# Projecting all queries first in a fused attention and FFN kernel

## The reference, cut to what matters

```python
x = x + xattn(layernorm(x), ctx, mask, Wq, bq, Wk, bk, Wv, bv, Wo, bo)
# att = scale * q k^T;  att * mask - 1e10 * (1 - mask);  softmax;  @ v;  @ Wo + bo
t = layernorm(x)
h = relu(t @ w1[0] + b1[0]);  y = t + h @ w2[0] + b2[0]
x = x + layernorm(y) * gamma + beta
```

## Time and profile before

| | us |
|---|---|
| median of 3 runs (lowest, highest) | 248.0 (247.46, 249.1) |
| the profiled execution, device time | 246.66 |
| its span, first to last instruction | 244.9 |
| TensorE busy | 208.8 (85%) |
| VectorE busy | 149.8 (61%) |
| ScalarE (ACT) busy | 120.9 (49%) |
| GpSimd busy | 80.2 (33%) |
| mean granted TensorE clock | 0.941 |
| moved by DMA | 26.09 MB |

### The profile page before, as it was taken

One profiled execution on the slowest core, in us unless ns is written; L12 is line 12 of the kernel. 1 busy time (PEld: TensorE's weight loads), 2 busy tenths in 40 slices (PEclk: granted clock), 3 DMA queues, 4 the chain that ended last, 5 costly groups with the idle time before them and its releaser, 6 DMA issues.

```text
span 244.9 us, 3545 instructions
## 1 busy us (share of the span) xinstructions
PE 208.8 (85%) x1273; PEld 159.0 (65%) x1273; DVE 149.8 (61%) x354; ACT 120.9 (49%) x210; POOL 80.2 (33%) x88
## 2 busy tenths in 40 slices
PE   0378779459968999996999999999999999889990
PEld 0273757145613775484779876898777899878890
DVE  1989478836651697442338865826858426885464
ACT  2442932326636447677632648744755850158200
POOL 5627617130410041824101732321541441460010
PEclk9999955959995799999999999999999999999998
DMA  6963679857767707593072434000410100011011
GB/s 180 364 212 77 182 175 244 223 173 190 174 152 215 167 19 130 139 197 118 5 160 78 111 66 107 3 3 26 106 45 4 43 0 3 0 43 43 3 43 43
DMA packets 18098, 26.09 MB, mean 107 GB/s; under 512 B 2441, under 2 KB 9393, under 8 KB 18081
## 3 DMA queue, kind: packets, MB, share of 16 engines
q1 hardware_dynamic: 15024, 20.85, 34.5%
q10 hardware_dynamic: 3057, 5.02, 6.9%
HBM read 14.92 MB, written 8.72 MB: 97 GB/s over the span
## 4 chain that ended last, share of the span: by engine, by line
PE 61%; DMA 14%; DVE 12%; SPq 3%; issue 3%; ACT 2%; ACTq 2%; POOL 1%; POOLq 0%
PE T L674 7%; PE acc L686 6%; DMA Sq<-nmx 5%; PE W L736 5%; PE W L738 5%; PE M L654 5%; PE W L737 5%; PE W L753 4%; PE W L750 4%; PE W L751 4%; DMA Sq<-mD 3%; PE W L695 3%; SPq L520 2%; DMA xin<-in_x_dram 2%; DMA Mq<-qh 2%
## 5 line engine op out<-in xcount | busy, mean ns | idle before, releaser
L839 ACT ACTIVATE PT<-T 77x512 f32<-77x512 f32 x64 | 35.1, 592 | 35.8 <-PE T L674 28.3
L750 PE MATMUL W<-w2h,hh 128*128 128x256 f32 x128 | 36.5, 285 | 0.4 <-ACT hh L883 0.4
L994 DVE TENSOR_REDUCE mx<-M 128x6 f32<-128x462 f32 (+1 forms) x48 | 26.1, 580 | 17.4 <-PE M L654 17.1
L753 PE MATMUL W<-w2h,hl 128*128 128x256 f32 x128 | 36.2, 283 | 0.2 <-DVE hl L1057 0.2
L751 PE MATMUL W<-w2l,hh 128*128 128x256 f32 x128 | 36.0, 281 | 0.0
L674 PE MATMUL T<-Sq,KS 128*77 128x512 f32 x64 | 26.2, 470 | 6.3 <-ACT PT L839 3.7
L879 ACT ACTIVATE hr<-W,cols 128x512 f32<-128x512 f32 x32 | 22.1, 689 | 12.3 <-PE W L738 11.1
L654 PE MATMUL M<-KM,Mq 128*128 128x234 f32 (+1 forms) x96 | 21.3, 346 | 7.6 <-DMA Mq<-qh 6.5
L736 PE MATMUL W<-x2h,w1h 128*128 128x512 f32 x64 | 26.3, 410 | 1.5 <-DVE x2l L1051 1.5
L654 PEld LDWEIGHTS M<-KM,Mq 128*128 128x128 f32 (+1 forms) x96 | 17.9, 240 | 13.7 <-DMA Mq<-qh 7.9
L1176 POOL TENSOR_TENSOR hl<-hr,hh 128x512 fp32r<-128x512 f32 x12 | 15.5, 1288 | 33.0 <-ACT hh L883 33.0
(11 more groups left out here) (138 smaller groups left out, 408.0 us busy)
## 6 DMA issues: line engine op xcount, KB each, us to landing
Sq<-qD SPq DMA_DIRECT2D x16, 384.0 KB
qD<-qh ACTq DMA_DIRECT2D x16, 256.0 KB
xin<-in_x_dram SPq DMA_DIRECT2D x4, 512.0 KB, 8.6
qD<-ql SPq DMA_DIRECT2D x8, 256.0 KB
Mq<-qh SPq DMA_DIRECT2D x16, 96.0 KB, 4.5
out_dram<-xn SPq DMA_DIRECT2D x6, 256.0 KB, 2.2
Sq<-mD SPq DMA_DIRECT2D x1, 1280.0 KB, 8.2
w1raw<-in_L_ffn_w_dram SPq DMA_DIRECT2D x2, 512.0 KB, 8.8
```

Of the source, the lines that this page charges most:

```text
L750: e.matmul(y, hh[:, f, q:q + 128], w2h[:, f * E:(f + 1) * E], start=(f == 0), stop=False)
L753: i = e.matmul(y, hl[:, f, q:q + 128], w2h[:, f * E:(f + 1) * E], start=False, stop=(f == 7))
L839: e.activation(PT[:, m % 6, :], T[m % 2][0:TK, :], ACT.Exp).then_inc(exped, 1)
L994: e.tensor_reduce(heads, M[(nth[step] - 1) % 2][:, 0:w * KP].rearrange("p (g h t) -> p g h t", g=1 if s < 2 else 2, t=KP)[:, :, :, 0:TK], ...
```

## The change

- `x` and the output are laid out so that a partition holds four consecutive rows of a chunk (one packet of 4 KB for each partition); `x` of all chunks is loaded at the start.
- Biases, identity tables and the query bias come in one constant array of 476 columns made on the host, and the context comes already turned; the loads of biases, their turn (`rows`) and the context's (`ctx`) are gone. Constants, context, Wk and Wv are the first loads on ACT's queue.
- The query bias is added inside `qproj` by a third matmul against the mask's flag rows; `bqk` and the `single`, `low` tables are gone. `keys` are plain selections: one matmul per head for `KM` and two for `KS`, 48 in all (before 56).
- `norm`, `scale`, `turn` and `qproj` of all four chunks stand ahead, among the key tables and the maxima of chunk 0; `qh` has four slots, `xn` and `xnT` two per chunk parity. SP issues one write of the high part and one (`qlow`) of the low part per group; ACT issues none.
- `qD` holds two parts per head instead of three; a quad is two transfers (32 rows of high and low, and 16 of high again). For chunks 1 to 3 `qload` fetches the copy for the maxima from `qD`.
- `mxt` turns all 16 heads at once for chunks 1 to 3. The mask reload is in two halves per tile.
- `finish` is split into `centre` and `finish`. `kh` is made by ACT from PSUM.
- The table `TIMES` is new on every engine.

The diff, cut to its core:

```diff
-        "qproj": "14.2 16.0 / 34.3 36.5 / 56.5 58.8 / 88.6 107.1",
...
+        "qproj": "14.7 19.1 / 24.8 27.0 / 29.4 31.4 / 37.0 39.9",
+        "smax": ("22.4 22.6 24.4 26.8 28.9 29.2 33.3 34.9 35.1 36.8 38.9 39.2 / 42.1 42.3 43.2 43.9 45.3 45.7 46.2 46.7 "
+            "47.1 47.6 49.0 49.2 / 56.1 57.4 57.9 59.1 60.7 66.5 67.3 68.8 71.1 73.6 76.4 76.7 / 79.7 80.3 82.0 85.4 "
+            "91.4 91.6 95.0 95.3 102.3 104.2 106.8 107.0"),
+        "mxt": "36.0 42.7 / 50.8 / 85.6 / 110.5",
+        "st": ("39.4 39.6 41.8 42.5 43.4 43.6 45.5 46.0 46.9 47.3 49.4 49.7 50.5 51.2 53.0 53.3 / 54.5 54.7 56.4 56.6 "
+            "57.6 58.2 58.8 60.5 63.9 64.1 65.6 66.2 67.1 69.0 69.2 70.4 / 89.1 89.3 90.9 91.1 94.8 95.5 96.9 100.1 "
+            "100.3 102.1 102.5 103.9 107.2 110.9 111.6 113.6 / 119.2 120.8 122.9 124.7 128.3 128.5 131.7 132.0 135.2 "
...
+        "qproj": "22.4 30.4 / 31.0 31.5 / 32.2 40.7 / 45.3 62.6",
+        "qlow": "21.8 27.1 / 29.9 32.8 / 34.4 44.7 / 93.2 125.7",
+        "qload": "19.5 23.8 / 39.6 41.3 / 52.8 57.6 / 77.1 78.2",
+        "quadq": "35.0 37.8 43.0 47.0 / 50.8 54.5 58.7 60.9 / 79.3 81.5 92.1 100.6 / 113.1 114.8 128.1 132.4",
+        "quadm": "37.3 38.9 44.2 46.4 / 52.3 53.9 57.0 62.0 / 86.9 87.5 91.6 101.7 / 112.6 114.2 125.2 133.5",
+        "finish": "126.3 129.4 / 154.4 161.2 / 195.9 197.8 / 201.8 204.1 204.6 207.2",
...
-    if kind in ("qproj", "qload", "mxt", "attn"):
+    if kind == "mxt":
+        return [[(kind, c, g) for g in range(turns(c))] for c in range(NC)]
+    if kind in ("qproj", "qlow", "qload", "attn"):
...
+def turns(c):
+
+    return 2 if c == 0 else 1
...
-        mD = dram("mD", (QR, 1024))
-        qD = [dram(f"qD{c}", (H, 3, D, 512)) for c in range(NC)]
-
-        cst = sb("cst", [P, 164])
...
-        x_v = x.rearrange("b (n p) e -> p (b n) e", p=P)
-        o_v = out.rearrange("b (n p) e -> p (b n) e", p=P)
+        x_v = x.rearrange("b (m p n) e -> p (b m) n e", m=2, n=4)
+        o_v = out.rearrange("b (m p n) e -> p (b m) n e", m=2, n=4)
...
-            e.dma_start(xin[:, 0:4, :], x_v[:, 0:4, :]).then_inc(ld_x[0], 16)
-            e.dma_start(cst[:, :], const).then_inc(ld_c, 16)
-            e.dma_start(mrow[:, :, :], mask[0, 0].rearrange("(n p) t -> p n t", p=P)).then_inc(ld_m, 16)
+            e.dma_start(xin[:, 0:4, :], x_v[:, row0(0)]).then_inc(ld_x[0], 16)
+            e.dma_start(mrow[:, :, :].rearrange("p (m n) t -> p m n t", m=2),
+                        mask[0, 0].rearrange("(m p n) t -> p m n t", m=2, n=4)).then_inc(ld_m, 16)
+            e.dma_start(xin[:, 4:8, :], x_v[:, row0(1)]).then_inc(ld_x[1], 16)
             e.dma_start(wq[:, :, :], wview(Wq)).then_inc(ld_wq, 16)
-            e.dma_start(xin[:, 4:8, :], x_v[:, row0(1):row0(1) + 4, :]).then_inc(ld_x[1], 16)
+            for c in (2, 3):
+                e.dma_start(xin[:, 4 * c:4 * c + 4, :], x_v[:, row0(c)]).then_inc(ld_x[c], 16)
             for i in range(2):
...
                 elif kind == "qproj":
                     c, g = a
-                    qd = qD[c][8 * g:8 * g + 8]
+                    fresh.wait_ge(q_high, nth[step])
+                    e.dma_start(qD[c][8 * g:8 * g + 8, :, 0, :].rearrange("h d n -> (h d) n"),
+                                qh[:, 2 * (c % 2) + g, :].bitcast(F32)).then_inc(qh_out[2 * (c % 2) + g], 16)
+                elif kind == "qlow":
+                    c, g = a
                     fresh.wait_ge(q_split, nth[step])
-                    e.dma_start(qd[:, 1, :, :], ql[:, g, :].bitcast(F32)).then_inc(q_out[g], 16)
+                    e.dma_start(qD[c][8 * g:8 * g + 8, :, 1, :].rearrange("h d n -> (h d) n"),
+                                ql[:, g, :].bitcast(F32)).then_inc(ql_out[g], 16)
...
                 elif kind == "qload":
                     c, g = a
...
+                        e.dma_start(Mqf[Q0:Q0 + 32, 4 + g, :], qh[96:P, g, :].bitcast(F32)).then_inc(ms_ld[g], 16)
+                    else:
+                        fresh.wait_ge(qh_out[2 * (c % 2) + g], 16 * (c // 2 + 1))
+                        fresh.wait_ge(scored, nth["smax", c - 1, 3, 1])
+                        e.dma_start(Mqf[Q0:Q1, 2 * g:2 * g + 2, :],
+                                    qD[c][8 * g:8 * g + 6, :, 0, :].rearrange("(j h) d n -> (h d) j n", j=2)
+                                    ).then_inc(ms_ld[g], 16)
+                        e.dma_start(Mqf[Q0:Q0 + 32, 4 + g, :],
+                                    qD[c][8 * g + 6:8 * g + 8, :, 0, :].rearrange("h d n -> (h d) n")).then_inc(ms_ld[g], 16)
...
                 elif kind == "quadq":
                     c, k = a
                     u, s = quad(c, k), 4 * (k % 2)
...
+                        fresh.wait_ge(sq_static, 4 * u + 4)
+                    else:
                         fresh.wait_ge(st_made, 4 * (u - 1))
-                    e.dma_start(Sqf[QR:P, s:s + 4, :],
-                                qD[c][4 * k:4 * k + 4].rearrange("h r d n -> (r d) h n")).then_inc(sq_ld[u % 2], 16)
+                    heads = qD[c][4 * k:4 * k + 4]
+                    e.dma_start(Sqf[Q0:Q0 + 32, s:s + 4, :], heads.rearrange("h d r n -> (d r) h n")).then_inc(sq_ld[u % 2], 16)
+                    e.dma_start(Sqf[Q0 + 32:Q1, s:s + 4, :],
...
                 elif kind == "qproj":
                     c, g = a
                     fresh.wait_ge(xnT_made, 2 * nth["turn", c])
                     fresh.wait_ge(ld_wq, 16)
                     t = take(step)
-                    e.matmul(t[:, :], wq[:, 0, g * 128:(g + 1) * 128], xnT[:, 0, :], start=True, stop=False)
-                    e.matmul(t[:, :], wq[:, 1, g * 128:(g + 1) * 128], xnT[:, 1, :],
+                    e.matmul(t[:, :], wq[:, 0, g * 128:(g + 1) * 128], xnT[:, c % 2, 0, :], start=True, stop=False)
+                    e.matmul(t[:, :], wq[:, 1, g * 128:(g + 1) * 128], xnT[:, c % 2, 1, :], start=False, stop=False)
+                    fresh.wait_ge(bqr_made, 1)
+                    fresh.wait_ge(mT_made, half(c) + 1)
+                    e.matmul(t[:, :], bqr[:, g, :], mT[:, 512 * half(c):512 * half(c) + 512],
                              start=False, stop=True).then_inc(q_made, 1)
...
+                        fresh.wait_ge(*((km_made, m - 2) if m < 9 else (ks_made, m - 8)))
+                    fresh.wait_ge(*((k_high, g + 1) if to == "KM" else (k_split, g + 1)))
+                    for i, h in enumerate(range(3 * j, min(3 * j + 3, 8))):
+                        o = t[0:48, 2 * TK * i:2 * TK * (i + 1)]
                         high = kh[:, g, :, :].rearrange("p b t -> p (b t)")
-                        e.matmul(o, single[0:TK, 8 * g + h, :], low[0:TK, :, :].rearrange("p b t -> p (b t)"),
-                                 start=True, stop=False)
                         if to == "KM":
-                            i = e.matmul(o, once[:, h, :], high, start=False, stop=True)
+                            made = e.matmul(o, sel_m[:, h, :], high, start=True, stop=True)
                         else:
-                            e.matmul(o, twice[:, h, :], high, start=False, stop=False)
-                            i = e.matmul(o, once[:, h, :], kl[:, g, :, :].rearrange("p b t -> p (b t)"),
-                                         start=False, stop=True)
-                    i.then_inc(keys_made, 1)
...
                 elif kind == "mxt":
                     c, g = a
-                    fresh.wait_ge(maxed, 12 * c + (12 if g else 8))
+                    r = H // turns(c)
+                    fresh.wait_ge(maxed, 12 * c + (8 if turns(c) == 2 and g == 0 else 12))
                     t = take(step)
                     for n in range(4):
-                        i = e.transpose(t[0:8, n * 128:(n + 1) * 128], mx[:, n, 8 * g:8 * g + 8], ident)
+                        i = e.transpose(t[0:r, n * 128:(n + 1) * 128], mx[:, c % 2, n, r * g:r * g + r], ident)
                     i.then_inc(mx_turned, 1)
...
                 elif kind == "qproj":
                     c, g = a
+                    r = 2 * (c % 2) + g
                     fresh.wait_ge(q_made, nth[step])
-                    if c:
-                        fresh.wait_ge(q_out[g], 48 * c)
-                    fresh.wait_ge(x_turned, 2 * nth["turn", c])
-                    e.copy(qh[:, g, :], bank[step][:, :]).then_inc(q_high, 1)
-                    fresh.wait_ge(q_high, nth[step])
-                    for r in (0, 2):
-                        e.dma_start(qD[c][8 * g:8 * g + 8][:, r, :, :], qh[:, g, :].bitcast(F32)).then_inc(q_out[g], 16)
+                    if c > 1:
+                        fresh.wait_ge(qh_out[r], 16)
+                        fresh.wait_ge(q_split, nth["qproj", c - 2, g])
+                    if c == 2:
+                        fresh.wait_ge(ms_ld[g], 48)
+                    e.copy(qh[:, r, :], bank[step][:, :]).then_inc(q_high, 1)
...
                 elif kind == "mxt":
                     c, g = a
+                    r = H // turns(c)
...
-                elif kind == "finish":
```

(20 more changed lines are left out.)

517 lines of the change are left out of this document (243 added, 274 removed), and 171 rows, old and new, of the table TIMES.

## The result

The changed kernel takes **231.6 us** (median of 4 runs, 230.83 to 232.05) beside 248.3 for the kernel before (247.46 to 249.1): ratio **0.9325, 95% interval 0.9284 to 0.9367**, 16.7 us less. The forecast was 223.2 us, range 214 to 232. So the sign held, and the range too, by 0.4 us at its upper end; 8.4 us are missing. The profiled execution took 232.05 us, its span is 230.2.

What follows compares the result with a forecast made beforehand. It took DMA, VectorE and waits to bound the head and TensorE, with holes, the body. Head 46.5, body 168.9 and tail 4.7 make 220.1 us; 1.76 outside the span and 1.3 to the median give 223.2, range 214 to 232.

Steps and rivals of the forecast that it cites:

- Head: Start to first score matmul: VectorE's list, then the maxima's transfer, set it; 46.5 us, 6.2 less than before.
- (b): Head, bound by bytes: 10.0 MB moved before the first score matmul, at 205 GB/s 48.7 us.
- Rival 2: Head not shortened: work added to VectorE and queues eats the gain, 52.7 us stays, total 229.4; chance 0.15.
- rival 1: Head: SP's queue drowns in query transfers ahead of the maxima, total 249 to 251 us, slower than before; chance 0.03.
- projections moved (-8.7): Body: chunks 2 and 3 no longer projected there, where TensorE is saturated; 4.35 us saved for each.
- one turn (-1.3): Body: chunks 1 to 3 turn their maxima once instead of twice, three blocks of 0.44 us less.
- ACT's issue and the half clock (-7.7): Body: ACT issues no query writes, so waits for exponentials (3.2 us) and the half clock after (4.5 us) go.
- the low part of x (-1.5): Body: TensorE's 1.5 us wait for chunk 3's low part goes, by splitting centre from finish and reordering; 0 to -1.5.
- the tail's centring (-0.5): Tail: one VectorE step, the centring, now lies beside GpSimd's root, saving 0.5 us.
- DMA for the second attention chunk (+2, range 0 to +10): Body, 46 to 70 us: 5.95 MB at 205 GB/s take 29 us, 5 late, partly beside matmuls.
- The second way: Whole kernel: the code's table of due times plus 9 us lag, with tail and rest, gives 221.4 us.
- Rivals 2 and 3: 2: head not shortened, 229.4 us, chance 0.15; 3: TensorE at half clock from 40 to 75 us, +8, 231 us, chance 0.13.

Runs made afterwards that it cites:

- Experiment 9: Maxima of chunks 1 to 3 turned in two halves again, on the version with on-chip mask copies: 223.17 us, beside 221.46 for its pair.
- Experiment 8: Chunk 3's norm, scaling, turn and projection put later, behind the first scores, on the version with on-chip mask copies: 224.58 us, ratio 0.907.
- experiment 7: Kernel before the change without its mask reload, so part of the computation is left out: 244.69 us, ratio 0.9863.
- Experiment 6: Kernel before the change with only the writes of the queries' high part issued by SP instead of ACT: 251.93 us, ratio 1.0178.
- experiment 5: Changed kernel with the writes of the queries' high part issued by ACT again, one per group: 232.15 us, ratio 0.9374.
- experiment 10: Changed kernel with the centring joined to the finish again, behind GpSimd's root: 237.54 us, beside 231.65 for its pair.
- experiment 1: Changed kernel without the mask reload, chunks 2 and 3 using the first half's mask (part of the computation left out): 221.23 us, ratio 0.8947.
- experiment 3: Changed kernel with the second half's mask rows copied on chip by GpSimd instead of reloaded by DMA: 221.73 us, and 221.46 us run again.
- Experiment 4: Changed kernel with the mask reload written to all 128 partitions instead of 77, 3.67 MB instead of 2.2: 238.1 us, ratio 0.9588.

## Why the prediction was right, and where it was wrong

**The time.** The range held at its edge, and partly by luck. The forecast gave the profiled execution 221.9 us, and it took 232.05, 10.1 more: 11.5 us missing in the body, 1.7 given back by the head. The median then lies 0.4 us below that execution, where the forecast put it 1.3 above, which gives back as much again and says nothing about the change. The stretch that the forecast held likeliest, 217 to 228, was missed. Of its signs, the first score matmul (44.8), the queries' writes off ACT, the exponentials (no wait) and the tail (just under 5 us) came as said. The granted clock of 1.0 from 60 us on and the body of 166 to 172 us did not.

**Head: right, 44.8 for 46.5, with one term too long.** The last maximum of the first eight heads, SP's issue of the transfer, and the first score matmul:

```profile
40.62 0.48 DVE L1005 TENSOR_REDUCE mx<-M 128x4 f32<-128x308 f32 x1
42.41 0.71 SPq L570 DMA_DIRECT2D Sq<-nmx  x1
44.81 0.43 PE L689 MATMUL T<-Sq,KS 128*77 128x512 f32 x1
```

VectorE's part ends at 41.1 us (the sum has 40.9). From SP's issue on it is 2.4 us, where the sum has 0.6 and 4. The bytes of (b) were right as well: 226 GB/s over 44.8 us are 10.1 MB, forecast 10.0, but the rate of 205 was too low, so its 48.7 us did not bind. Rival 2 (a head of 52.7) falls. SP did stand on its issues (runs of four and two query writes took 3.44 and 4.49 us at 32 to 40 us), without delaying the maxima past the forecast, so rival 1 falls too.

**Body, projections moved (-8.7) and one turn (-1.3): the second is borne out, the first not measured alone.** Experiment 9 has the turn at 1.5 us. Experiment 8 puts one of the two projections back and is slower by 2.9, by the clock as much as by the matmuls. The body without the reload is 169.1 us, and it would be wrong to lay that beside the forecast's 168.9: this has a reload in it, at +2 us, and a reload of the kernel before, worth about 3 us (experiment 7), in its 186.1. Taken out of both, the forecast would be some 164 us. So the other terms together promised up to 5 us more than came, and the runs don't say which of them.

**Body, ACT's issue and the half clock (-7.7): gone as forecast, but worth less by itself.** The waits for exponentials and the half clock of 73 to 83 us are gone. Experiment 6 bears out the cause in the old order: with SP issuing, both go. But the kernel is then 4 us slower, not 7.7 faster, since TensorE waits for the tokens' scaling (10.1 us) and the maxima (6.9 us) instead. And in the new order ACT can issue again without harm (experiment 5, 0.33 us each). What differs there is one write per group instead of two, and that nearly all of them are issued ahead of the scores; which of the two matters was not tried.

**Body, the low part of x (-1.5), and the tail's centring (-0.5).** The wait for the low part is gone, and the tail's gain is 0.6 (experiment 10). What the forecast doesn't have is what the split is worth inside the new order: 5.9 us, 5.1 of them in the body, because there a joined block stands on VectorE between attention's own steps. This is not a gain on the kernel before, whose joined block stood elsewhere in the order and cost 1.5 us of waits.

**Body, DMA for the second attention chunk (+2, range 0 to +10): this is the step that failed.** "At 205 GB/s it takes 29 us, 5 late, of which some lies beside matmuls." The sum under it is wrong. A quad is 0.39 MB, as the forecast's own head has it, so four are 1.57 MB and not 3.1, and 4.4 MB were due in these 24 us, not 5.95. The trace agrees: 178 GB/s from 46 to 70 us are 4.3 MB. At 205 GB/s 4.4 MB take 22 us, and nothing is late; the +2 came out of a mistake, and the right sum of bytes would have given 0. The bytes did arrive, and still TensorE waited. It waited not for queries but for one transfer of 8 KB at the end of the chain, which took 5.4 us in full engines; and the same happened again with the second half of the reload, from 95 to 109 us, for which the forecast has no term.

By experiment 1 the reload costs the body **11.3 us** (180.4 against 169.1), made up of 7.1 us of waits for the maxima and 4.4 us more of TensorE busy time (200.2 against 195.8), the half clock behind them; in the medians it is 10.4, and 10.2 against the copies of experiment 3. The mean rate of 205 failed too: in the stages of the first wait the full engines moved 141 to 167 GB/s. Experiment 4 puts that down to the narrow transfers (197 GB/s for 385), without showing that a faster reload would have been cheaper.

The copies of queries for the maxima, which now come from DRAM and which the forecast counts as nothing, have 2.6 us of TensorE's waits; those of the kernel before have 6.5.

**Tail: 5.0 for 4.7.**

**The second way** (the table's due times plus a lag of 9 us) gave 221.4 and failed at the same place: the lag is 5.4 us at the first score matmul and about 21 at the last FFN block. A table without rates of the DMA says nothing about a transfer that does not keep up.

**Rivals 2 and 3** gave 229.4 and 231, near to what was measured, and neither is what happened: the head was shortened by more than forecast, and the half clock was there for some 10 us, not 35, and as the consequence of a wait.

## What to carry to other kernels

Sum up the DMA of a stage by kind of transfer, each at the rate that rows show for its width in partitions, and not at the mean of the queue, and hold the sum against the bytes of the whole kernel, where a term counted twice shows. Then ask which small transfer at the end of a chain has to get through those engines. What an order keeps covered in one place (a reload beside FFN matmuls) can be the bound in another. Here the remedy was to bring constant data back by a copy on an idle engine of the chip. And a step that waits for another engine can be dear by what stands behind it in its engine's list, so every place where it occurs counts, not only the last.

## What the runs showed of the hardware that was not expected

- Full DMA engines (share 1.05 to 1.14) moved 141 to 201 GB/s in stages of a reload into 64 and 13 partitions beside queries, and 132 at a share of 1.07 with queries into 16 to 48 partitions alone. With the reload into all 128 they moved 265 to 327 GB/s at a share of 0.86 to 1.12.
- A transfer of 8 KB took 5.4 and 6.6 us on SP's queue and 4.7 to 7.7 us on ACT's where TensorE waited for it. In the head of the changed kernel, at a DMA share of 0.19, the first score followed its issue by 2.4 us.
- In the changed kernel TensorE was busy for 0.57 and 0.59 us of the two stages from 63 to 67 us, fell to 1.2 GHz, and was there until about 72 us although it then worked without a pause. With one projection less ahead of the first scores (1.05 of 2 us busy) it was there from 42 to 51 us.
- A pair of VectorE steps of 128 x 256 took 2.96 us beside GpSimd, where it took 0.80 alone.
